# First graph layer multiplied by its bases before the adjacency, with weights, sums, weight ring and results placed anew

## The reference, cut to what matters

```python
# layer 0, graph part: 20625 edges, 8 relations, 4 bases
W = einsum('rb,bio->rio', comp, basis)
out = segment_sum(einsum('ni,rio->nro', x, W)[src, etypes], dst, n) + x @ loop_weight + bias
# layer 0, mix: linear attention, layernorm, relu MLP, layernorm; added to the graph part
# layer 0, experts: top 2 of 8 experts, hidden size 1024
# layer 1, graph part: bases = node @ W_bases, then symmetric, sum and max aggregation of bases[src]
aggregated = stack([agg_sym, agg_sum, agg_max])      # max over the incoming edges of a node
h = einsum('nhk,nkf->nhf', weightings, aggregated)   # then a graph norm and relu
# layer 1, mix: linear attention with batch norm
# layer 1, experts: top 2 of 64 experts, hidden size 512
```

## Time and profile before

| what | us |
|---|---|
| median of 3 runs (987.62 to 994.85) | 991.87 |
| the profiled execution | 991.11 |
| its span | 989.4 |
| PE busy | 711.3 (72%) |
| DVE busy | 485.5 (49%) |
| POOL busy | 198.0 (20%) |
| ACT busy | 161.1 (16%) |
| mean granted TensorE clock | 0.863 |

### The profile page before, as it was taken

One profiled execution on the slowest core, in us unless ns is written; L12 is line 12 of the kernel. 1 busy time (PEld: TensorE's weight loads), 2 busy tenths in 40 slices (PEclk: granted clock), 3 DMA queues, 4 the chain that ended last, 5 costly groups with the idle time before them and its releaser, 6 DMA issues.

```text
span 989.4 us, 13447 instructions
## 1 busy us (share of the span) xinstructions
PE 711.3 (72%) x4912; PEld 522.4 (53%) x4912; DVE 485.5 (49%) x1173; ACT 161.1 (16%) x355; POOL 198.0 (20%) x213
## 2 busy tenths in 40 slices
PE   2467767989979619999747789787333597878880
PEld 1355646877868519999545456444212244444440
DVE  7537888656663451111343265588686522222231
ACT  0311311224201104233000021111100011111110
POOL 3000000000000011231503545372200332232213
PEclk9978977899989759999658999898855699999995
DMA  3440100000000066998631355465251499999922
GB/s 110 91 135 1 50 1 1 1 2 1 2 1 2 9 203 215 326 321 277 181 109 37 98 135 155 110 181 141 82 219 62 128 381 410 410 410 410 410 84 72
DMA packets 84500, 147.75 MB, mean 149 GB/s; under 512 B 10961, under 2 KB 57641, under 8 KB 84428
## 3 DMA queue, kind: packets, MB, share of 16 engines
q1 hardware_dynamic: 58438, 84.97, 25.5%
q0 software_dynamic: 18336, 55.09, 16.5%
q10 hardware_dynamic: 7654, 6.75, 2.0%
HBM read 127.45 MB, written 19.31 MB: 148 GB/s over the span
## 4 chain that ended last, share of the span: by engine, by line
PE 48%; DVE 21%; DMA 14%; issue 4%; POOL 3%; ACT 1%; DVEq 1%; POOLq 0%; SPq 0%; ACTq 0%
DMA big<-xn_rows,spots 11%; PE ps L1271 6%; PE ps L1127 5%; PE ps L1141 5%; PE ps L932 5%; DVE arena L1640 4%; PE ps L819 3%; PE ps L978 3%; PE ps L1382 3%; PE ps L1405 2%; DVE arena L2389 2%; PE ps L943 2%; PE ps L918 2%; DVE big L1916 2%; DVE ya L1640 2%
## 5 line engine op out<-in xcount | busy, mean ns | idle before, releaser
L670 POOL DMA_INDIRECT big<-xn_rows,spots x46 | 45.1, 981 | 432.4 <-DVE spots L2047 409.1
L978 PE MATMUL ps<-big 125*128 125x144 bf16 x825 | 94.7, 242 | 19.8 <-DVE big L1640 11.6
L1640 DVE TENSOR_TENSOR arena<-arena,ps 125x400 f32 x110 | 57.9, 526 | 90.4 <-PE ps L980 80.2
L978 PEld LDWEIGHTS ps<-big 125*128 125x128 bf16 x825 | 84.5, 107 | 25.8 <-DVE big L1640 14.4
L1271 PE MATMUL ps<-arena,early 125*128 125x512 bf16 (+1 forms) x315 | 77.2, 402 | 21.7 <-DVE arena L2389 16.3
L980 PE MATMUL ps<-big 125*128 125x64 bf16 x825 | 92.6, 205 | 0.0
L980 PEld LDWEIGHTS ps<-big 125*128 125x128 bf16 x825 | 81.9, 104 | 6.7 <-issue 4.3
L1640 DVE TENSOR_TENSOR big<-ps,b1cols 128x512 f32<-128x512 f32 x32 | 22.1, 691 | 116.9 <-PE ps L1391 116.9
L2389 DVE TENSOR_TENSOR_SCAN arena<-arena,ps 128x512 f32<-128x512 bf16 (+1 forms) x41 | 51.6, 1257 | 47.5 <-PE ps L1287 36.1
L1271 PEld LDWEIGHTS ps<-arena,early 125*128 125x128 bf16 x315 | 31.1, 104 | 62.6 <-DVE arena L2389 19.6
L1382 PE MATMUL ps<-arena,big 128*64 128x512 f32 x256 | 63.7, 619 | 0.0
(11 more groups left out here) (356 smaller groups left out, 1108.0 us busy)
## 6 DMA issues: line engine op xcount, KB each, us to landing
arena<-in_L_ffn_W_dram SPq DMA_DIRECT2D x53, 1024.0 KB, 10.2
arena<-in_L_ffn_W_dram POOLq DMA_DIRECT2D x39, 1024.0 KB, 16.5
rtab<-arena SPq DMA_DIRECT2D x40, 256.0 KB, 3.9
arena<-new_node SPq DMA_DIRECT2D x40, 128.0 KB, 3.3
ys<-big ACTq DMA_DIRECT2D x32, 128.0 KB, 7.3
arena<-src_list SPq DMA_DIRECT2D x20, 125.0 KB
arena<-in_L_mix_W_dram SPq DMA_DIRECT2D x2, 1024.0 KB, 6.9
fys<-big ACTq DMA_DIRECT2D x14, 128.0 KB, 3.1
```

Source lines behind the costliest of these rows:

```text
L978: pe.matmul(psflat[:, at:at + K2 * WIN], ohs[:, s, u, t * TP:t * TP + 128], pieces[:, 0:K2 * WIN], start=first and t % 2 == 0, stop=False, ...
L1640: return v.tensor_tensor(out, p, q, op)
```

## The change

Six things change.

1. **Graph layer.** `project(q)`, q from 0 to 9, now multiplies row tiles by bases, two (basis, tile) products at a time, at groups 25 to 32; ACT copies each product to SBUF (`keep_projected`), where all twenty stay in regions that are free then. `aggregate(part, i)` multiplies an adjacency tile by product i and adds it in bank 7: part 0 three i for each group from 27 on, part 1 four i for each group from 49 on, part 2 in one row after the loop.
2. **Weights behind the fetch.** SP waits for all ten gathers of layer 0's results before it issues the weight sets 0 and 1.
3. **Sums in the loop.** The neighbour sums of tiles 0 and 1 follow block 0 of the scan loop, those of tiles 2 to 4 blocks 1 to 3; the query product moves from block 3 to 4 on PE and from 4 to 5 on DVE. The two tests on PE are one. `btab` is stored in five DMAs, one for each tile.
4. **Ring of seven.** Two more sets lie in SBUF that is free by then (`rows` and `mixw`, `turned2` and `kept2`, which hold several smaller buffers of before). SP loads sets 2 to 6 when `c_out` is 17, except the last megabyte, which waits for the rows' store and for `spots`. The store of `xn_rows` moves to ACT.
5. **Results by tiles.** The ending gathers `ya` and `yb` of a tile in turn, adds them by tile, and stores the output by tile.
6. Some semaphores are merged, and a small buffer is placed in another.

```diff
+PROJECT_AT = (25, 25, 26, 26, 27, 28, 29, 30, 31, 32)
+PROJECT_IN = (7, 6, 7, 6, 6, 6, 6, 6, 6, 6)
...
+        ew.append([rows[:, 0:8, :].rearrange("p (e a) d -> p e (a d)", e=2),
+                   mixw[:, 0:2048].rearrange("p (e n) -> p e n", e=2)])
+        ew.append([turned2[:, 0:2048].rearrange("p (e n) -> p e n", e=2),
+                   kept2[:, 0:2048].rearrange("p (e n) -> p e n", e=2)])
+        RING = len(ew)
...
+            for k in range(2):
+                sp.wait_ge(y_got[k], 80)
             for s in range(2):
                 sp.dma_start(ew[s][0], w1v[s]).then_inc(ew1_loaded[s], 16)
...
             for s in range(2, RING):
                 sp.dma_start(ew[s][0], w1v[s]).then_inc(ew1_loaded[s], 16)
-                sp.dma_start(ew[s][1], w2v[s]).then_inc(ew2_loaded[s], 16)
-            sp.wait_ge(norm_ready, 6)
-            sp.dma_start(node_major(xn_rows[1].ap()), xn[:, :, :]).then_inc(xn_stored, 16)
+                if s < RING - 1:
+                    sp.dma_start(ew[s][1], w2v[s]).then_inc(ew2_loaded[s], 16)
+            sp.wait_ge(xn_stored, 32)
+            sp.wait_ge(spots_out, 2)
+            sp.dma_start(ew[RING - 1][1], w2v[RING - 1]).then_inc(ew2_loaded[RING - 1], 16)
...
-            sp.wait_ge(o_ready, NT)
-            sp.dma_start(node_major(a["out"]), x[:, :, :]).then_inc(o_stored, 16)
+                for t in range(NT):
+                    sp.wait_ge(sparse_done, t + 1)
+                    sp.dma_start(a["out"][t * TP:(t + 1) * TP, :], x[:, t, :]).then_inc(o_stored, 16)
...
-            fetch(ys)
+            for t in range(NT):
+                for k in range(2):
+                    pool.indirect_dma_start((ya, yb)[k][:, t, :], None, ys.ap(), ...
...
+            def project(q):
+                pe.wait_ge(m_out, 16 if q == 0 else 17)
+                if q >= 2:
+                    pe.wait_ge(g_out, q - 1 if q < 4 else q)
+                for i in (2 * q, 2 * q + 1):
+                    for k in range(KD):
+                        m = pe.matmul(ps[0:TP, PROJECT_IN[q], i % 2 * D:(i % 2 + 1) * D],
+                                      xnT[:, k, i % NT * TP:(i % NT + 1) * TP], basis[:, i // NT, k, :],
+                                      start=(k == 0), stop=(k == KD - 1))
+                m.then_inc(g_mm, 1)
+
+            def aggregate(part, i):
+                if i == 0:
+                    pe.wait_ge(flushed, READY[part] if part < 2 else EG)
+                    if part:
+                        pe.wait_ge(p_added, part)
+                b, s = i // NT, i % NT
+                pe.wait_ge(g_out, max(i // 2 + 1, 4))
+                for t in range(t0, t1):
+                    m = pe.matmul(ps[0:TP, 7, (t - t0) * D:(t - t0 + 1) * D], adj5[:, b, s, t * TP:(t + 1) * TP],
+                                  projected[i], start=(i == 0 and t == t0), stop=False, skip_group_check=True)
...
                 for b in range(NMB):
                     messages(b)
                     if b >= 2:
                         turn_runs(b - 2)
-                    if b == 3:
+                    if b == 0:
+                        neighbour_sums(0)
+                        neighbour_sums(1)
+                    if 1 <= b < NT - 1:
+                        neighbour_sums(b + 1)
+                    if b == 4:
                         attend_queries()
...
+            def keep_projected(q):
+                act.wait_ge(g_mm, q + 1)
+                for i in (2 * q, 2 * q + 1):
+                    m = nc.scalar.copy(projected[i], ps[0:TP, PROJECT_IN[q], i % 2 * D:(i % 2 + 1) * D])
+                m.then_inc(g_out, 1)
...
-            act.wait_ge(c_out, 5)
-            act.dma_start(node_major(btab.ap()), bas[:, :, 0:DB]).then_inc(btab_stored, 16)
+            for t in range(NT):
+                act.wait_ge(c_out, t + 1)
+                act.dma_start(btab.ap()[t * TP:(t + 1) * TP, :], bas[:, t, 0:DB]).then_inc(btab_stored, 16)
...
+            for t in range(NT):
+                dve.wait_ge(y_tile[t][0], y_tile[t][1] + 32)
+                done(v.scalar_tensor_tensor(out=x[:, t, :], in0=ya[:, t, :], scalar=gate[:, t, 2:3], in1=x[:, t, :],
+                                            op0=ALU.mult, op1=ALU.add))
+                v.scalar_tensor_tensor(out=x[:, t, :], in0=yb[:, t, :], scalar=gate[:, t, 3:4], in1=x[:, t, :],
+                                       op0=ALU.mult, op1=ALU.add).then_inc(sparse_done, 1)
```

More of the change, by code:

```diff
@@ L934, in aggregate @@
-                m.then_inc(g_mm, 1)
-            def project(part, b):
-                t0, t1 = PARTS[part]
-                pe.wait_ge(g_out, part * 8 + KD * (b + 1))
-                if b == 0 and part:
-                    pe.wait_ge(p_added, part)
-                for t in range(t0, t1):
-                    for c in range(KD):
-                        m = pe.matmul(ps[0:TP, 7, (t - t0) * D:(t - t0 + 1) * D],
-                                      gT[b % 2][:, c, (t - t0) * TP:(t - t0 + 1) * TP], basis[:, b, c, :],
-                                      start=(b == 0 and c == 0 and t == t0), stop=False, skip_group_check=True)
-                m.then_inc(g_used, 1)
@@ L963, in _ @@
             order += [(19 + t, lambda t=t: attended(t)) for t in range(NT)]
-            order += [(READY[0] + 1 + i // 2, f) for i, f in enumerate(part_steps(0))]
+            order += [(at, lambda q=q: project(q)) for q, at in enumerate(PROJECT_AT)]
+            order += [(READY[0] + 1 + i // 3, lambda i=i: aggregate(0, i)) for i in range(NB0 * NT)]
             order += [(35, lambda: mixed_turn(0)), (36, lambda: mixed_turn(1))]
@@ L967, in _ @@
             order += [(43 + t, lambda t=t: mixed(t)) for t in range(NT)]
-            order += [(READY[1] + 1 + i // 2, f) for i, f in enumerate(part_steps(1))]
+            order += [(READY[1] + 1 + i // 4, lambda i=i: aggregate(1, i)) for i in range(NB0 * NT)]
             def clear(banks, parts):
@@ L1019, in _ @@
                 pe.nop()
-            for step in part_steps(2):
-                step()
+            for i in range(NB0 * NT):
+                aggregate(2, i)
             moe = dict(h=0, y=0, r=0)
@@ L1200, in _, with neighbour_sums @@
             cproduct(m)
[L1201 to L1204 removed]
+            def neighbour_sums(t):
+                pe.wait_ge(c_out, 7 if t < 2 else 7 + t - 1)
                 for s in range(NT):
@@ L1299, in _ @@
                 pe.wait_ge(l_out, 16)
-            pe.wait_ge(p_out, 2)
-            slow = pe.value_load(loose[0:1, 0:1], min_val=0, max_val=E)
-            with pe.If(slow > 0):
                 for d in range(NT):
@@ L1328, in _ @@
             with pe.Else():
+                nc_[0] = products
                 pe.wait_ge(split_ready, 1)
@@ L2236, in _, with neighbour_sums @@
             m.then_inc(c_out, 1)
-            for t in range(NT):
+            def neighbour_sums(t):
                 dve.wait_ge(c_mm, 7 + t)
@@ L2335, in _ @@
             with dve.If(slow > 0):
+                for t in range(NT):
+                    neighbour_sums(t)
+                dve.wait_ge(c_out, 12)
                 weigh(0, 8)
@@ L2368, in _ @@
                 dve.wait_ge(mx_turned, 1)
-                for t in range(NT - 2):
-                    mark_free(v.memset(held[:, :], 0.0))
                 mark_free(v.tensor_copy(agg[:, 0:4, 2 * DB:3 * DB],
```

153 lines of the change are left out of this document (76 added, 77 removed).

## The result

The changed kernel takes 950.48 us (median of 4 runs, 948.51 to 956.28) against 991.38: a ratio of 0.9598, 95% interval 0.9542 to 0.9653. The forecast was 948.4. The profiled execution took 951.46 us with a span of 949.4; the mean granted clock is 0.868 (0.863 before).

The account below looks back on a forecast made before the run. PE was taken to bound the graph layer and scan loop's start, DMA the experts, gather landings being the chain's largest piece. -17 - 0.5 - 7 - 13 - 6 = -43.5 us against a median of 991.87 gave 948.4; range 937 to 968.

Parts of the forecast that it names:

- A: Graph layer: products made once and added straight into bank 7, without copies in PE's chain; about -17 us, bounds -12 and -19.
- Rival 2: Graph layer: projections run at half clock throughout groups 25 to 32, 17.3 us more, total 965; chance 0.08.
- B: Weights behind the fetch: DVE's wait for the second half of the fetched rows goes; -0.5 us, bounds 0 and -3.
- C: Scan loop's start: neighbour sums fill PE's gaps around the messages, two tests become one; -7 us, bounds -3 to -9.
- Rival 1: Scan loop: sums are not absorbed and each delays a scan, only the branch's gap is won; total 954, chance 0.13.
- D: Experts: seven weight sets mean fewer loads in the busy stretch and a shorter PE tail; -13 us, bounds -5 and -17.
- 2 x 5.73 = 11.5 us fewer: Experts: 25 instead of 27 sets loaded in the stretch, so the last transfer ends about 930.5 instead of 942.
- rival 3: Experts: gathers stay last to land behind second weights in POOL's queue, the tail returns; -3, total 958, chance 0.12.
- E: Ending: only the last tile's adds and a 128 KB store follow the last landing; -6 us, bounds -4 and -7.
- Rival 4: Experts, 790 to 940 us: two more sets outstanding lower the weights' rate; slower, 1002 at 300 GB/s, chance 0.04.

Follow-up runs that it names:

- noC: The changed kernel with all five neighbour sums ahead of the test and scan loop again, the single test kept: 950.65 us, ratio 0.9626.
- before_1test: The kernel before the change with PE's two tests of one number made one, neighbour sums left in place: 989.45 us, ratio 0.9998.
- ring5: The changed kernel with the two new weight sets taken out, so five sets again: 958.99 us, ratio 0.9690.
- w2sp: The changed kernel with the second weights of sets 7 to 31 on SP's queue instead of POOL's: 942.73 us, ratio 0.9530.
- before_w2sp: The kernel before the change with only the second weights of sets 5 to 31 moved from POOL's queue to SP's: 984.30 us, ratio 0.9941.
- noA: The changed kernel with the graph layer's old order (adjacency times rows, copy, times basis) put back: 968.53 us, ratio 0.9810.
- late_proj: The changed kernel with the graph layer's projections up to two groups later, the first at group 27: 957.76 us, ratio 0.9665.

## Why the prediction was right, and where it was not

**A** held in mechanism and size. Part 0 was to end 0.7 us later than before and ended 0.4 earlier (216.76, 217.19 before); part 1 was put at 304 and ended at 301.91; part 2 was put at 10 us with a slower clock and took 10.4 at 0.84. What the forecast had wrong was a bound, not the value: it read the clock 0.50 of 165 to 175 as something that the products would meet. They were the work that took it away. Rival 2 (products at half clock) fell with the same rows.

**B** was right in being nearly nothing.

**C** came out 2.2 us better, by another working than told; that the size was near is in part luck. The forecast had the sums fall into the gaps ahead of and behind the messages, the stop among them, and two tests become one. But noC shows 5.5 of the 8.95 us, and -7.4 for the stage, without moving a sum, and before_1test shows that the number of tests was not why the stop went. Rival 1 (each sum in the loop delays a scan, C = -1) did not come: with the sums in the loop the seventh messages end 3.4 us earlier than without.

**D** is the term that was mis-sized: -4.80 for -13. The rate stayed what was said, 410 GB/s, but two steps of the working fell short. The first is "2 x 5.73 = 11.5 us fewer": the last weights land 163.5 us after the first gather instead of 170.4, 6.9 us sooner. The two sets did bring most of it (10.1 us, ring5 against after), but 3.2 us went at the start of the stage (before against ring5), where the forecast put nothing: it had the extra loads behind 727 us in a quiet stretch, and the last megabyte went out 0.7 us ahead of the first gather.

The second is "PE can follow the last transfers by some 12 us instead of the 21.4 us that it needed after its last wait". The 21.4 count from the last wait for a gather and the 12 from the last transfer; counted alike, from the landing of the last weights, PE's end was 12.7 us behind before and is 14.8 in after. The reason is in two numbers that the forecast had as one: a set's bytes take 5.73 us at 411 GB/s, and four iterations of the chain took 22.92, the same per set; so "landing and bytes say the same". With seven sets they part: the bytes still need 5.73, the chain 24.98 / 4 = 6.25, as POOL's queue, in which the gathers and second weights stand, gets less of the rate. After its last wait for a gather, which ends at 894.12, PE needed 30.4 us. The forecast's test, "wrong if gathers land later than 23 us", was met, and what came is rival 3, with a size between the two: the -5 that was D's lower bound. w2sp confirms it, since taking the weights out of the gathers' queue brings 8.4 us, and before_w2sp shows that the same queue cost before some 6 us already.

**E** came out at -7.35 for -6: the forecast allowed 5.0 us behind the last landing and 4.0 were needed. The store of a tile is 2.96 us where it allowed 3.1 from the earlier trace rows; most of the difference is the 1.1 us that it set beside the adds and the store. The Trainium skill's rule on a DMA's fixed and byte parts (DMA: Bandwidth & Descriptors, "Anatomy of one DMA", a section on GpSimd's path) gave 2.9 as an estimate; this store went out on SyncE's queue, and the trace agrees. For the whole store the estimate of 6.7 is short of the 7.3 to 7.7 measured.

Rival 4 (the weights' rate falls) did not come: 410 GB/s in 800 to 880.

## What to carry to other kernels

A landing time under a full DMA load measures the queue in front of the transfer, not the transfer: ask which queue a small gather shares with large loads before giving it more buffers or the loads a deeper ring. When two limits show the same period, a change that relieves one says nothing of the other; price both apart. Two queues that share a full load each take their part: here a deeper ring let one run ahead with loads that nobody waited for, and the queue that the work waited for got less (191 GB/s instead of 204). And work that can run ahead pays twice where it lies in an engine's waits: here the early products left part 0 ending where it had (216.76 us, 217.19 before) and ended the half-clock stretch around them.

## What was not expected of the hardware

- Filling TensorE's waits raised the granted clock: 165 to 175 us had PE busy 6.54 to 6.55 of 10 at 0.50 in three kernels (before, noA, late_proj) and 10.00 at 0.91 in after.
- Small row gathers land in some 6 us while the DMA engines move 407 GB/s, if no weights stand ahead of them in their own queue; in line with weights they took 17 to 32 us at the same rate.
- A stop of about 5 us at a test and branch behind a semaphore wait, against 1.15 us where that wait stood elsewhere. A 16 KB packet on an instruction queue lies inside the long stop and ahead of the short one; its part in it is argued, not isolated.
